# Graph attention by edges: at most two row gathers under way, on two alternating semaphores

## The reference

```python
h = (x @ W.T).reshape(N, H, C)              # H = 4 heads of C = 64
e = leaky_relu(a_s[src] + a_d[dst], 0.2)
p = exp(e - m[dst])                          # m: the largest e of each target
alpha = p / (denom[dst] + 1e-16)
out = segment_sum(alpha[:, :, None] * h[src], dst, num_segments=N)
```

## Time and profile before

| what | value |
|---|---|
| median of 3 runs | 4284.76 us (4278.98 to 4286.46) |
| the profiled execution, first to last instruction | 4872.5 us |
| instructions in it | 63960 |
| TensorE busy | 3544.1 us, 73% |
| VectorE busy | 2671.7 us, 55% |
| ScalarE busy | 1621.1 us, 33% |
| GpSimd busy | 1291.4 us, 27% |
| gathers of the edge loops (L836) | 850, 832.8 us busy |

### The profile page before, as it was taken

One profiled execution on the slowest core, in us unless ns is written; L12 is line 12 of the kernel. 1 busy time (PEld: TensorE's weight loads), 2 busy tenths in 40 slices (PEclk: granted clock), 3 DMA queues, 4 the chain that ended last, 5 costly groups with the idle time before them and its releaser, 6 DMA issues. The chain is left out here.

```text
span 4872.5 us, 63960 instructions
## 1 busy us (share of the span) xinstructions
PE 3544.1 (73%) x22446; PEld 2944.2 (60%) x22446; DVE 2671.7 (55%) x6836; ACT 1621.1 (33%) x4188; POOL 1291.4 (27%) x1348
## 2 busy tenths in 40 slices
PE   3365556667345455576988999997999879969796
PEld 3244444456334333465775888887457879968795
DVE  5465556754445555557865888887212533344444
ACT  1133333311122232334553666665111122321131
POOL 6454454245354455400000000000000022210063
PEclk8676667778667677788999999998999989989898
DMA  5233333233433333344500000003455431135324
GB/s 152 78 101 98 101 108 90 82 102 98 110 91 101 98 109 107 92 109 131 135 9 5 1 1 1 1 1 76 110 126 139 154 107 37 37 84 136 131 71 123
DMA packets 178027, 419.54 MB, mean 86 GB/s; under 512 B 58688, under 2 KB 103410, under 8 KB 177216
## 3 DMA queue, kind: packets, MB, share of 16 engines
q1 hardware_dynamic: 116800, 251.73, 18.6%
q0 software_dynamic: 60928, 164.04, 11.7%
HBM read 331.25 MB, written 84.36 MB: 85 GB/s over the span
## 5 line engine op out<-in xcount | busy, mean ns | idle before, releaser
L836 POOL DMA_INDIRECT sb<-features,sb x850 | 832.8, 980 | 785.9 <-DVE sb L901 540.6
L2054 PE MATMUL ps<-sb 128*128 128x125 f32 x5184 | 635.6, 279 | 71.2 <-DVE sb L2118 70.1
L2054 PEld LDWEIGHTS ps<-sb 128*128 128x128 f32 x5184 | 595.0, 192 | 111.8 <-DVE sb L2118 110.5
L3447 ACT ACTIVATE sb<-ps,sb 128x128 f32<-128x128 f32 x784 | 220.1, 376 | 572.5 <-PE ps L3373 500.4
L1194 PE MATMUL ps<-sb 128*125 128x128 bf16 x850 | 117.1, 286 | 395.0 <-PEq L1192 188.1
L2085 ACT ACTIVATE sb<-ps 128x125 f32<-128x125 f32 x1296 | 330.0, 272 | 223.7 <-PE ps L2054 194.9
L3373 PE MATMUL ps<-sb 128*128 128x128 f32 x3136 | 393.2, 282 | 12.7 <-DVE sb L3418 8.5
L1205 PE MATMUL ps<-sb 128*125 128x260 f32 x1700 | 394.1, 391 | 9.9 <-PEq L1203 6.2
L545 DVE TENSOR_SCALAR sb<-sb 128x782 bf16<-128x782 f16 x425 | 188.2, 493 | 373.8 <-PE ps L619 162.8
L3387 PE MATMUL ps<-sb 128*128 x1568 | 373.5, 385 | 19.5 <-issue 10.3
L3373 PEld LDWEIGHTS ps<-sb 128*128 128x128 f32 x3136 | 377.7, 198 | 16.3 <-DVE sb L3418 11.0
(11 more groups left out here) (357 smaller groups left out, 5493.9 us busy)
## 6 DMA issues: line engine op xcount, KB each, us to landing
sb<-adj SPq DMA_DIRECT2D x125, 683.6 KB
neg<-sb SPq DMA_DIRECT2D x25, 683.6 KB
adj<-sb SPq DMA_DIRECT2D x25, 683.6 KB
sb<-neg SPq DMA_DIRECT2D x25, 683.6 KB
sb<-rows_y SPq DMA_DIRECT2D x30, 560.0 KB
sb<-in_L_ffn_W SPq DMA_DIRECT2D x16, 1024.0 KB
sb<-features,sb POOLq DMA_INDIRECT x850
sb<-adj SPq DMA_DIRECT2D x125, 79.3 KB
```

What stands on the lines that cost most here:

```text
L836: e.indirect_dma_start(hgs[i % 4][:, w, :], None, k.HR, indirect(ids[i % 3][:, w:w + 1])).then_inc(*hg_in[i % 4].by(16))
L2054: return e.matmul(sums(n, g)[:, 0, :], V[:, y, (4, 0, 5, 1, 2, 3)[g], :], self.old_h(n)[:, y, :], start=False, stop=y == 1, skip_group_che ...
L3447: m = e.activation(hts[n % 2][:, c, :], hidden(n, c), ACT.Gelu, bias=cons[n % 4][:, c:c + 1])
```

## The change

In the edge loops gathers no longer count on a semaphore for each buffer, but alternate between two by their running number n = 17 i + w. Before gather n is issued, GpSimd waits until all gathers before n-1 that used the same semaphore have landed, which is until gather n-2 has landed. Those who read a block's rows, or overwrite its indices, wait on both semaphores for the count at the block's end (`gathered`).

```diff
-        eg_in, hg_in = k.sigs("eg_in", 6), k.softs("hg_in", 4)
+        eg_in, hg_in = k.sigs("eg_in", 6), k.softs("hg_in", 2)
...
+        def gathered(e, b):
+            n = W * (b + 1)
+            e.wait_ge(*hg_in[0].at(16 * ((n + 1) // 2)))
+            e.wait_ge(*hg_in[1].at(16 * (n // 2)))
...
                     for w in range(W):
+                        n = W * i + w
+                        if n >= 2:
+                            e.wait_ge(*hg_in[n % 2].at(16 * (n // 2)))
                         e.indirect_dma_start(hgs[i % 4][:, w, :], None, k.HR,
-                                             indirect(ids[i % 3][:, w:w + 1])).then_inc(*hg_in[i % 4].by(16))
+                                             indirect(ids[i % 3][:, w:w + 1])).then_inc(*hg_in[n % 2].by(16))
...
                     if b >= 3:
-                        e.wait_ge(*hg_in[(b - 3) % 4].at(16 * W * ((b - 3) // 4 + 1)))
+                        gathered(e, b - 3)
...
-                    e.wait_ge(*hg_in[b % 4].at(16 * W * (b // 4 + 1)))
+                    gathered(e, b)
```

## The result

The changed kernel takes 4631.87 us (median of 4 runs, 4626.3 to 4638.03), the kernel before 4284.51 (4 runs, 4278.98 to 4286.46): ratio 1.081, 95% interval 1.080 to 1.083, so 8% slower. The forecast was slower, 4455 us, in a range from 4320 to 4560. The direction is right; the time lies 177 us above the forecast and 72 above the range.

The account below looks back on a forecast made before the run. GpSimd's gather issue was taken to be at or near the bound: 21.8 + 2.7 (landing) + 1.1 (collisions) = 25.6 us per block against 22.2, 3.4 more over 50 blocks, 170 us, 4455 us; range 4320 to 4560.

Parts of the forecast that it names:

- GpSimd's issue is the bound in the timed run: In the edge loops, gather issue at 21.8 us per block was put at or near the bound of the timed run.
- 22.2 us for a timed block: Length taken for one block of the edge loops in the timed run before the change, between 21.8 and 22.5 us.
- the missing 588 us: The profiled execution, 4872.5 us, exceeded the timed median, 4284.8; most of the difference was placed in the edge loops.
- The waits released by the gathers' own landing: Sign in the profile after: GpSimd's gaps before its gathers would be ended by the landing of earlier gathers.
- GpSimd's idle time before indices: Sign in the profile after: GpSimd's idle time until a block's indices come would fall from 540.6 to some 350 us.
- a row of 17 gathers: Sign in the profile after: one block's 17 gathers in the edge loops would spread over 24 to 27 us.
- No change: Rival: the edge loops have slack in the timed run too, hiding the longer gathers; 4293 us, chance 0.11.
- slower by less: Rival: gathers land sooner in the timed run, so only collisions with other transfers cost; 35 us, 4320 us, chance 0.13.
- the step of the landing: Gather n to n+2 would take 2.82 us (2.71 to 3.04) against 2.50: 2.7 us more per block (1.8 to 4.6).
- the loss by collisions: Beside SyncE's matrix writes in every other block, held gathers lose time not made up: 1.1 us per block (0.3 to 1.6).
- the late signals as a product of the profiling: In the edge loops VectorE waits 501 us for matmuls long ended; profiling was blamed, and for most of the missing 588 us.
- The rival "faster": If gathers hold up TensorE's signals in timed runs too, fewer under way give time back: 75 us, 4210 us, chance 0.06.

Follow-up runs that it names:

- e12: The kernel before, unedited, profiled on a chip where it takes about 4285 us: 4284.66 us.
- e2: The changed kernel with one semaphore, so each gather waits for the one before to land; on a chip where the kernel before takes about 4877 us: 5913.19 us.
- e1: The kernel before, unedited, profiled once more, on a chip where it takes about 4877 us: 4874.31 us.
- e5: The changed kernel, unedited, on a chip where the kernel before takes 4877.91 us: 4660.12 us, ratio 0.956.
- e17: The kernel before with a 128x256 fill of a spare tile ahead of each gather, no waits for landings; slower kind of chip: 4534.94 us, ratio 0.930.
- e14: The kernel before with gathered rows of 528 bytes in place of 1,056, on a chip where the kernel before takes 4874.11 us: 5025.76 us, ratio 1.030.
- ring of three: The changed kernel with three semaphores in turn, each gather waiting for the last but two; three runs on the slower kind of chip: 4708.89, 4725.58, 4732.63 us.
- e16: The kernel before with a 128x160 fill of a spare tile ahead of each gather, on the slower kind of chip: 4872.17 us, ratio 0.999.
- e9: The kernel before with gathered rows of 528 bytes in place of 1,056, on a chip where the kernel before takes about 4285 us: 4430.19 us, ratio 1.033.
- e10: The kernel before with a 128x64 fill of a spare tile ahead of each gather, on a chip where the kernel before takes about 4285 us: 4294.37 us, ratio 1.002.
- e13: The kernel before with a 128x64 fill of a spare tile ahead of each gather, on the slower kind of chip: 4878.74 us, ratio 1.000.

## Why the prediction was right in its sign and wrong in its size

**Right: GpSimd's issue is the bound in the timed run.** The prediction took 22.2 us for a timed block from the missing 588 us; e12 has 22.0. This was partly luck, since the reason given for the missing time was false (below). The waits released by the gathers' own landing and spread as the one that waits are as written. GpSimd's idle time before indices, which was to fall to some 350 us in the profile, is 3.7 us, and a row of 17 gathers takes 27.3 us from first to last start, where 24 to 27 were named. "No change" and "slower by less" are out on the first kind: the block has no slack, and 95% of the pairs of gathers take 2.98 us or more, start to start.

**Wrong: the size of the step of the landing, 2.82 us per pair.** The changed kernel needs 3.03 (lower quarter of its pairs; the median is 3.10), and e2 finds 3.05 for one landing by itself. The upper bound, 2.77 + 0.27 = 3.04 from the earlier trace rows, was the right value. The prediction took a value nearer to the packets, since L950's own start lies in the 2.77. The trace now has both parts: the landing is signalled 2.79 us after the start (median), and the held gather starts 0.26 us later. Against 2.50 this is 8.5 x 0.53 = 4.5 us per block, not 2.7.

**Wrong: the loss by collisions, 1.1 us (0.3 to 1.6).** The mean pair step is 3.44 us after and 2.59 before, in all 0.855 x 8.5 = 7.3 us per block. Less the 4.5 of the landing, 2.8 are left, more than the upper bound. The prediction counted only the matrices' writes in one of two blocks, by the packets they displace. They show (blocks of one parity are 30.7 us long, of the other 27.7), but they are only half of it: what the pairs take over 3.03 us falls in about equal parts to some 95 pairs beside these writes (4.7 to 4.9 us in the mean) and to the some 750 others (3.27 us), and 36% of all pairs take over 3.3 us. Each landing that is late holds the next start back, and nothing is made up later. The late ones are those beside which other queues are carrying data, the edge loop's own loads and writes too (the count of landings in the section on the result). Before, such a delay went unseen: there, too, the packets ended later in the mean than in the median (2.9 against 2.5 us in e12). That the other transfers cause the delay, and do not only stand beside it, no run tried.

With 4.5 and 2.8 in the prediction's own sum: 22.0 + 7.3 = 29.3 us per block, 50 x 7.3 = 365 us, 4650 against the 4631.87 measured. The step that failed is thus the price of a held gather in both of its terms, 2.7 and 1.1 us per block put for 4.5 and 2.8; the mechanism stands.

**Wrong: the late signals as a product of the profiling.** They belong to chips of the second kind, in timed runs too (e1, and 4877 us in all groups there). The size that was drawn from them, 22.2 us per block, came out right only because the missing 588 us are mostly what these signals cost in these same loops (517 us between e1 and e12). The Trainium skill's rule that emitting a record costs an engine zero cycles ("NOTIFIC — the notification-queue block", Constraints, capacities, measured rates) was set against the 588 us. The runs agree with the page as far as they can tell: 4874.31 us for the profiled execution against a median of 4877.0 on one chip, 4284.66 against 4285.63 on another.

**The rival "faster" holds on the second kind.** It was given 0.06 for "earlier signals, if TensorE's signals are held up by gathers in the timed run too". That is what e5 shows, 4.4% faster. Its mechanism needs one correction. It isn't the number under way: the full fill has three or more under way at 174 of 850 issues (e17) and clears much of the signals; half rows land earlier, have three or more under way at 145 (e14), and clear none. What goes with the late signals is how closely GpSimd issues gathers: 1.25 to 1.36 us apart throughout the block takes 32.5 to 33.0 us, 1.44 apart 26, and with two under way the mean distance is 1.7, though a fifth of the single steps there are still under 1.28 (e5). Whether it is the mean pace, or the pauses in between, no run separates. The ring of three, irregular in its distances, stands between (29.3 to 30.0). So the change trades late signals for a slower issue: on a chip with the first it gains 218 us, on a chip without it loses 347.

The prediction also said what the changed kernel's profile would show where a block has 12 us of slack: GpSimd's idle time down to some 350 us and the span nearly unchanged. In e5 the idle time before indices is 5.2 us and the span 213 us shorter than e1's, since with the late signals the slack goes too.

**Open.** Why a chip is of the one or the other kind; by what way close issue on GpSimd keeps TensorE's signals back; and whether the matmuls themselves end later than the records say, which no view here can tell from a late signal; why every other block suffers more. How the loss on the first kind divides into its two terms rests on the traces, since no run with another number under way fell there. No kernel here was shown to beat the kernel before on both kinds. The full fill, which helps on the second (4527), was not run on the first, where 17 x 0.19 us per block of added issue should make it some 160 us slower (argued).

## What to carry to other kernels

Before the times of one table and one trace are put in one sum, see that the profiled execution's own time fits the times: where it doesn't, ask first whether both are from the same chip, and make no argument from the difference. Then, a wait for a landing costs what its waiter sees (start to start, here 3.0 us for a gather that issues in 1.25), not what the packets show, and once an engine at the bound is held, each late landing is lost for good; price it by the mean landing, not the median. Limiting the transfers under way paid here only where something else suffered from their close issue, and there spacing them out bought more (4527 against 4660 us).

## What the runs showed of the hardware

- The same kernel takes 4285 us on some chips and 4875 on others, at 0.4% from lowest to highest within a group at most, and most of the difference lies where GpSimd issues gathers: from first to last gather of both loops 1096.4 us (e12) against 1613.5 (e1), 517 of the 590 us between the spans.
- While GpSimd issues gathers 1.25 to 1.36 us apart on the second kind, a hand-over from TensorE to ScalarE or VectorE, as the records tell it, can take 18 to 23 us (e16). ScalarE's reads over 3 us late are 57 of 250 in e1 and 38 in e16; at 1.44 us there are 23, the longest 10.2 us (e17); with two under way none (e5).
- A gather of 128 rows of 1,056 bytes is signalled as landed 2.79 us after its start (median, changed kernel), and a gather that waits for it starts 3.05 us after that start (median, e2). The Trainium skill's formula for one transfer issued by GpSimd ("DMA: Bandwidth & Descriptors", Anatomy of one DMA — SWDGE (gpsimd) path) gives 2.31 us by estimate; the traces have more, and they decide. Half the bytes move the packets' end from 2.5 to 2.2 us (medians, e12 and e9).
- A fill of 128x64 between two gathers takes 0.166 us and lengthens the distance from 1.25 to 1.28 us only (e10, e13); between two issues GpSimd is otherwise idle for 0.30 us.
